# Stacked router logits, expert 3's second layer moved up, and a reordered fill and first round

## The reference, cut to what matters

```python
x = x + _L0_gnn_ref(_layernorm(x), adj, W, a)     # elu(softmax(mask(leaky(f_i + f_j))) @ (x @ W))
x = x + _L0_ffn_ref(_layernorm(x), ...)           # six experts of three layers, top 2 by a router
x = x + _L1_gnn_ref(_layernorm(x), adj, W, a)
x = x + _L1_ffn_ref(_layernorm(x), ...)           # eight experts, routed by graph; then a layernorm
```

```python
rh = relu(features @ router_w1 + router_b1)                  # 128 -> 64
expert_logits = softmax(rh @ router_w2 + router_b2)          # 64 -> 6
top_w, top_i = top_k(expert_logits, 2)
routing_weights = softmax(top_w)
h1 = relu(einsum('bsd,edh->bseh', features, expert_w1) + expert_b1)
h2 = relu(einsum('bseh,ehf->bsef', h1, expert_w2) + expert_b2)
expert_out = einsum('bsef,efo->bseo', h2, expert_w3) + expert_b3
```

## Time and profile before

| | us |
|---|---|
| median of 3 runs (583.07 to 584.28) | 583.71 |
| the profiled execution | 578.58 |
| its span in the trace | 576.8 |

### The profile page before, as it was taken

The page is one execution under the profiler, slowest core; times in us unless marked ns, Lnnn a source line. Parts: engine busy times, 40 slices in busy tenths (PEclk is TensorE's granted clock), DMA queues, the critical chain, the costliest instruction groups (busy, mean ns, idle before and its releaser), DMA issues.

```text
span 576.8 us, 14978 instructions
## 1 busy us (share of the span) xinstructions
PE 541.0 (94%) x3752; PEld 448.3 (78%) x3784; DVE 451.5 (78%) x1664; ACT 417.7 (72%) x1097; POOL 228.9 (40%) x441
## 2 busy tenths in 40 slices
PE   6678999999999999999999999999987999999993
PEld 5556678787777887878777787867765799999993
DVE  3866969889898888989889897786557387877777
ACT  1355667878878787887878878786663678888883
POOL 5112214442443434334442434413313045666664
PEclk8899999999999999999999999999999899999998
DMA  8504325042340513415043250321320467887732
GB/s 205 121 15 151 99 67 167 3 165 71 96 151 13 165 44 121 125 39 165 11 153 88 77 165 2 110 70 44 110 74 2 145 206 221 260 259 221 219 114 73
DMA packets 78833, 66.44 MB, mean 115 GB/s; under 512 B 9916, under 2 KB 64460, under 8 KB 78796
## 3 DMA queue, kind: packets, MB, share of 16 engines
q1 hardware_dynamic: 65562, 60.60, 34.4%
q10 hardware_dynamic: 13234, 5.42, 3.5%
HBM read 61.57 MB, written 4.42 MB: 114 GB/s over the span
## 4 chain that ended last, share of the span: by engine, by line
PE 79%; issue 6%; DVE 5%; POOL 4%; ACT 3%; ACTq 1%; DMA 1%; DVEq 0%; POOLq 0%; SPq 0%
PE bank L1566 14%; PE bank L1553 13%; PE wide L206 5%; PE bank L1848 5%; PE wide L1848 4%; PE bank L1858 4%; PE wide L1858 4%; PE wide L239 4%; PE bank L1545 3%; PE bank L1546 3%; PE bank L1547 3%; PE wide L231 2%; PE wide L1594 2%; PE wide L199 2%; PE wide L220 2%
## 5 line engine op out<-in xcount | busy, mean ns | idle before, releaser
L1566 PE MATMUL bank<-w,h2w 128*128 128x128 f32 x768 | 104.2, 279 | 2.6 <-DVE h2w L1130 2.6
L1566 PEld LDWEIGHTS bank<-w,h2w 128*128 128x128 f32 x768 | 94.8, 192 | 7.9 <-DVE h2w L1130 4.0
L1553 PE MATMUL bank<-h,w 128*128 128x512 f32 x192 | 98.8, 596 | 0.3 <-ACT h L846 0.3
L841 ACT ACTIVATE h<-bank,b 128x512 f32<-128x512 f32 x96 | 66.2, 689 | 42.2 <-PE bank L1553 42.2
L846 ACT ACTIVATE h<-bank,b 128x512 f32<-128x512 f32 x96 | 65.9, 687 | 12.8 <-PE bank L1547 12.6
L1130 DVE TENSOR_TENSOR h2w<-h,wide_w 128x512 f32<-128x512 f32 x96 | 64.8, 676 | 8.0 <-ACT h L841 7.8
L1545 PE MATMUL bank<-xnTh,w1h 128*128 128x512 f32 x96 | 67.0, 698 | 0.0
L100 POOL TENSOR_TENSOR route_var_eps<-route_mean_var,eps 128x4 f32<-128x4 f32 x17 | 11.2, 659 | 117.5 <-DVE route_mean_var L93 117.3
L100 POOL TENSOR_TENSOR at_var_eps<-at_mean_var,eps 128x4 f32<-128x4 f32 x32 | 12.4, 387 | 95.4 <-DVE at_mean_var L93 95.2
L268 ACT ACTIVATE at_pr<-at_lk,at_nm 128x128 f32<-128x128 f32 x124 | 40.0, 415 | 1.7 <-DVE at_nm L303 1.5
L206 PE MATMUL wide<-at_wc,at_xT 128*128 128x130 f32 x248 | 34.8, 286 | 4.2 <-ACT at_xT L247 4.2
(11 more groups left out here) (304 smaller groups left out, 1363.6 us busy)
## 6 DMA issues: line engine op xcount, KB each, us to landing
wide_w<-w_scratch SPq DMA_DIRECT2D x96, 256.0 KB, 4.5
mask<-in_L_ffn_W SPq DMA_DIRECT2D x124, 128.0 KB, 2.4
x<-in_x SPq DMA_DIRECT2D x16, 256.0 KB, 5.4
adj_in<-in_adj SPq DMA_DIRECT2D x16, 256.0 KB, 6.0
wide_w<-bmix_scratch SPq DMA_DIRECT2D x16, 256.0 KB, 3.5
xin<-in_x SPq DMA_DIRECT2D x15, 256.0 KB, 5.8
out<-at_pr ACTq DMA_DIRECT2D x8, 256.0 KB, 2.8
out<-at_prT ACTq DMA_DIRECT2D x7, 256.0 KB, 2.9
```

Of the source, the lines that this page charges most:

```text
L841: a.activation(h2[:, e % 2, :], b_h2[:, :], ACT.Relu, bias=b2[:, e:e + 1]).then_inc(h2_ready, 1)
L1553: pe.matmul(b_h2[:, :], w2[:, e, :], h1[:, e % 2, :], start=True, stop=True).then_inc(l2_done, 1)
L1566: last = pe.matmul(b_out[:, s], h2w[:, e % 2, s], w3[:, e, :], start=False, stop=(e == E0 - 1), skip_group_check=True)
```

## The change

**Logits of stacked tiles.** The first router weights now stand twice side by side (128 columns instead of 64), so the hidden layer comes out twice, on partitions 0 to 63 and 64 to 127. `route_relu` takes tiles 0 and 1 from the lower half and tiles 2 and 3 from the upper half, in two activations of 64 by 256 instead of one of 64 by 512. rh then holds two tiles one above the other in 128 rows by 256 columns, and rw2 has the second weights twice on its diagonal with zeros beside them, so `route_logits` needs two products of 12 columns instead of four of 6. The second bias is no longer a row of rh; VectorE adds it in a new first step of `route_first` (`lgb`). The later steps count one more, which renumbers their semaphore values.

**Second layer of expert 3.** TensorE's `layer2(n + 3, 3)` moves from behind the transposes of the probabilities to a place between the logits and them, in every round from i0 = 1.

**Fill.** The router of group 0 starts earlier: `route_transpose` moves ahead of the rows of group 1's attention and its hidden layer is cut into a high and a low part, the high one ahead of the scores; it writes to another bank (b_out). The unread products in round -1 become 28, 5, 2 and 8 instead of 12, 3, 3 and 0. VectorE places the bias rows of two tiles in `split_b3` and of the other two (`place_b3(2, GG)`) behind the first `norm_apply` of the router. ScalarE's `relu2(0)` of group 0 moves behind the elu.

**First round.** Experts run ahead of each other in another order: `layer3(0)`, `layer2(2)`, `layer1(3)`, `layer3(1)` come before the scores of group 2, and `weigh(2)` and `weigh(3)` come earlier on VectorE. VectorE's statistics of group 1 for the router move ahead of the rescaling of the projection, and GpSimd's root of them ahead of the splits.

**Transfers.** b2, w2 and w3 move from ScalarE's queue to SyncE's, behind b3 and ahead of the late weights. ScalarE issues two more small ones (rb1 and the second router weights twice), and waits before them for a memset of rw2 by GpSimd.

The diff, cut; left out are the new shapes of the tiles, the semaphore counts, and the lines of round 0 and of the other engines that only follow the words above:

```diff
-            sp.wait_ge(b3_zero, 1)
+            sp.wait_ge(b3_zero, 2)
             for q in range(3):
                 sp.dma_start(b3[32 * q:32 * q + KW, :],
                              A["L0_ffn_expert_b3"].unsqueeze(1).broadcast_to([E0, GG, P])).then_inc(small_loaded, 16)
+            with nc.allow_non_contiguous_dma(reason="bias columns, once"):
+                sp.dma_start(b2[:, :], A["L0_ffn_expert_b2"].rearrange("e p -> p e")).then_inc(small_loaded, 16)
+            sp.dma_start(w2[:, :, :], A["L0_ffn_expert_w2"].rearrange("e d h -> d e h")).then_inc(small_loaded, 16)
+            sp.dma_start(w3[:, :, :], A["L0_ffn_expert_w3"].rearrange("e d h -> d e h")).then_inc(small_loaded, 16)
...
+            p.memset(rw2[:, :], 0.0).then_inc(b3_zero, 1)
...
+                if i0 == 0:
+                    norm_root(rn, p, eps, minus_half, 1, rn["xn_ready"])
                 if live("attn0", i0) and i0 != -LEAD["attn0"]:
                     attn_pool_split(at0, p, zero, i + 2)
-                if i0 == 0:
-                    norm_root(rn, p, eps, minus_half, 1, rn["xn_ready"])
...
-                a.dma_start(rb1[:, :], A["L0_ffn_router_b1"].unsqueeze(1)).then_inc(small_loaded, 16)
-                a.dma_start(rw2[0:RH, :], A["L0_ffn_router_w2"]).then_inc(small_loaded, 16)
-                a.dma_start(rw2[RH:RH + 1, :], A["L0_ffn_router_b2"].unsqueeze(0)).then_inc(small_loaded, 16)
+                a.wait_ge(b3_zero, 1)
+                for q in range(2):
+                    half = slice(q * RH, (q + 1) * RH)
+                    a.dma_start(rb1[half, :], A["L0_ffn_router_b1"].unsqueeze(1)).then_inc(small_loaded, 16)
+                    a.dma_start(rw2[half, q * E0:(q + 1) * E0], A["L0_ffn_router_w2"]).then_inc(small_loaded, 16)
+                a.dma_start(rb2[:, :], A["L0_ffn_router_b2"].partition_broadcast(P)).then_inc(small_loaded, 16)
                 a.dma_start(b1[:, :], A["L0_ffn_expert_b1"].rearrange("e p -> p e")).then_inc(small_loaded, 16)
                 a.dma_start(h2[:, 0, 0:RH], A["L0_ffn_router_w1"]).then_inc(raw_loaded, 16)
                 a.dma_start(h1[:, :, :].rearrange("p a f -> p (a f)")[:, 0:E0 * P],
                             A["L0_ffn_expert_w1"].rearrange("e d h -> d e h")).then_inc(raw_loaded, 16)
-                a.dma_start(b2[:, :], A["L0_ffn_expert_b2"].rearrange("e p -> p e")).then_inc(small_loaded, 16)
-                a.dma_start(w2[:, :, :], A["L0_ffn_expert_w2"].rearrange("e d h -> d e h"))\
-                    .then_inc(small_loaded, 16)
-                a.dma_start(w3[:, :, :], A["L0_ffn_expert_w3"].rearrange("e d h -> d e h"))\
-                    .then_inc(small_loaded, 16)
...
-                    a.activation(rh[0:RH, :], b_misc[0:RH, :], ACT.Relu, bias=rb1[:, :]).then_inc(rh_ready, 1)
+                    for q in range(2):
+                        half = slice(q * RH, (q + 1) * RH)
+                        part = a.activation(rh[half, :], of[half, lane[q]], ACT.Relu, bias=rb1[half, :])
+                    part.then_inc(rh_ready, 1)
...
-                    relu2(0, 0)
...
                 if i0 == -LEAD["route"]:
+                    relu2(0, 0)
                     relu1(1, 1)
                 elif live("experts", i0, 1):
                     relu1(n + 6, 0)
...
-                for t in range(GG):
+                place_b3(0, 2)
+
+            def place_b3(first, end):
+
+                for t in range(first, end):
                     v.tensor_scalar(b3x[0:64, t, :], b3h[0:64, :].bitcast(F32), rowtile[0:64, t:t + 1], None, ALU.mult)
                     v.tensor_scalar(b3x[64:KB, t, :], b3l[64:KB, :], rowtile[64:KB, t:t + 1], None, ALU.mult)\
                         .then_inc(split_step, 1)
...
-                lg = b_misc[:, 0:GG * E0].rearrange("p (t e) -> p t e", t=GG)
-                v.tensor_reduce(lgmx[:, :], lg, AX, ALU.max).then_inc(route_step, 1)
+                lg = b_misc[:, 0:GG * E0].rearrange("p (q h e) -> p h q e", q=2, h=2)
+                v.tensor_tensor(lgb[:, :, :].rearrange("p (h q) e -> p h q e", h=2), lg,
+                                rb2[:, :].unsqueeze(1).unsqueeze(1).broadcast_to([P, 2, 2, E0]), ALU.add)\
+                    .then_inc(route_step, 1)
                 v.wait_ge(route_step, base + 1)
-                v.tensor_tensor(lgd[:, :, :], lg, lgmx[:, :].unsqueeze(2).broadcast_to([P, GG, E0]),
+                v.tensor_reduce(lgmx[:, :], lgb[:, :, :], AX, ALU.max).then_inc(route_step, 1)
+                v.wait_ge(route_step, base + 2)
+                v.tensor_tensor(lgd[:, :, :], lgb[:, :, :], lgmx[:, :].unsqueeze(2).broadcast_to([P, GG, E0]),
                                 ALU.subtract).then_inc(route_step, 1)
 
...
+                if i0 == 0:
+                    measure(rn, 1, at0["x_ready"], 2)
+                    weight_low(0)
...
                 if i0 == 0:
-                    measure(rn, 1, at0["x_ready"], 2)
-                    weight_low(0)
...
+                if i0 == -LEAD["route"]:
+                    place_b3(2, GG)
...
+                if i0 == 0:
+                    weigh(3, 0, 3)
...
                 pe.wait_ge(xnTh_ready, g + 1)
+                pe.matmul(to[:, :], rw1h[:, :], xnTh[:, par, :], start=True, stop=False)
+                pe.matmul(to[:, :], rw1l[:, :], xnTh[:, par, :], start=False, stop=False)
+
+            def route_hidden_low(g, par, to=b_misc):
                 pe.wait_ge(xnTl_ready, g + 1)
-                pe.matmul(b_misc[0:RH, :], rw1h[:, :], xnTh[:, par, :], start=True, stop=False)
-                pe.matmul(b_misc[0:RH, :], rw1l[:, :], xnTh[:, par, :], start=False, stop=False)
-                pe.matmul(b_misc[0:RH, :], rw1h[:, :], xnTl[:, par, :], start=False, stop=True)\
...
             def route_logits(g):
                 pe.wait_ge(rh_ready, g + 1)
-                for t in range(GG):
-                    last = pe.matmul(b_misc[:, t * E0:(t + 1) * E0], rh[:, t * P:(t + 1) * P], rw2[:, :],
-                                     start=True, stop=True)
+                for q in range(2):
+                    last = pe.matmul(b_misc[:, q * 2 * E0:(q + 1) * 2 * E0], rh[:, q * P:(q + 1) * P], rw2[:, :],
+                                     start=True, stop=True, skip_group_check=True)
...
+                if i0 == 0:
+                    layer1(2, 0, 0, 2)
+                    bias3(0)
+                    layer3(0, 0)
+                    layer2(2, 2)
+                elif run:
+                    layer1(n + 1, i, par, 1)
...
                         pe.wait_ge(spread_step, 6)
-                    busy_fill(i0, 12)
+                    busy_fill(i0, 12 if i0 == -LEAD["attn0"] else 28)
+                    if i0 == -LEAD["route"]:
+                        route_transpose(i, i0)
                     attn_pe_rows(at0, pe, identb, i + 2)
-                    busy_fill(i0, 3)
-                if route and i0 != 0:
+                    busy_fill(i0, 3 if i0 == -LEAD["attn0"] else 5)
+                if route and i0 >= 0:
                     route_transpose(i, i0)
+                if i0 == -LEAD["route"]:
+                    route_hidden_high(0, 0, b_out)
+                    busy(b_pool, 2)
...
-                        layer1(0, 0, 1 - par, 0)
-
-                if run:
+                if route and i0 >= 0:
+                    pe.wait_ge(xnTl_ready, i + 2)
+                    route_hidden_high(i + 1, 1 - par)
+                    route_hidden_low(i + 1, 1 - par)
+                if i0 == -LEAD["route"]:
+                    route_hidden_low(0, 0, b_out)
+                    layer1(0, 0, 1 - par, 0)
+
...
                 if route:
                     route_logits(i + 1)
+                if i0 == 0:
+                    layer3(2, 2)
+                    layer2(4, 4)
+                if run and i0 > 0:
+                    layer2(n + 3, 3)
...
-                    busy_fill(i0, 16 if i0 == -LEAD["attn0"] else 0)
+                    busy_fill(i0, 16 if i0 == -LEAD["attn0"] else 8)
                     attn_pe_transpose_probs(at0, pe, ident, i + 2)
                     busy_fill(i0, 3)
 
-                if run:
-                    layer2(n + 3, 3)
+                if run and i0 > 0:
                     layer1(n + 4, i, par, 4)
```

131 lines of the change are left out of this document (68 added, 63 removed).

## The result

| | us |
|---|---|
| changed kernel, median of 16 runs (575.74 to 582.93) | 577.47 |
| kernel before, the 16 runs beside them (578.20 to 584.28) | 579.65 |
| ratio | 0.9946, interval 0.9923 to 0.9970 |

The account below looks back on a forecast made before the run. Steady rounds were taken as bound by TensorE's queue and a chain through ScalarE and VectorE arriving together, the fill by waits. First round -2.8, thirteen rounds -0.3, last round -0.4: 583.7 - 3.5 = 580.2 us, range 576.6 to 583.3.

Parts of the forecast that it names:

- the -2.8 for fill and first round: Fill through first round: earlier copies, exponentials and reordered experts bring the end of the first round 2.8 us earlier.
- the 583.7: Starting level: median of the runs of the kernel before, 5.1 us above its profiled execution, from which 3.5 was subtracted.
- The logits: Steady round, TensorE: two stacked products instead of four cost 0.41 of 0.81 us, so 0.40 goes.
- The two halves: Steady round, ScalarE: splitting the router's activation adds at most 0.15 us, hidden under a cover of 0.3 to 0.4.
- the second layer: Steady round: expert 3's second layer ahead of the transposes delays them by 0.86 us; 0.02 of the saved 0.40 remains.
- the 1.0: Start, ScalarE: with three issues moved away, the first copy starts at 8.00 instead of 9.05, 1.0 us earlier.
- 1.65 at the first mean: Fill, group 0: the front's 1.0 and four bias-row calls moved behind start VectorE's mean at 21.14 instead of 22.79.
- p_sum's 0.73 instead of 2.7: First round, VectorE: p_sum forecast at 54.4 instead of 57.06, 2.7 us earlier.
- Its own sign for being wrong: Prediction wrong if rounds get shorter than 24.3 us, or if the fill gains under 1.5 with the clock up.
- The second: Rival, fill: a low-clock stretch on the 28 unread products, or late bias rows, leaves 1.5 gain; 581.9 us; 20 in 100.
- The third: Rival, rounds: logits pair as long as four makes the exponential 0.35 later in each of 13; 585.1 us; 6 in 100.
- The first: Rival, rounds: copy and exponential keep their distance to TensorE's shortened queue, 0.35 gained each; 575.6 us; 12 in 100.

Follow-up runs that it names:

- l2_back: Changed kernel with expert 3's second layer put back behind the transposes of the probabilities from i0 = 1; 582.14 us, ratio to the kernel before 1.0013.
- l2_only: Kernel before with only expert 3's second layer moved up between logits and transposes from i0 = 1; 586.42 us, ratio 1.0099.
- rounds_only: Kernel before with stacked logits and expert 3's second layer moved up alone; loads, fill and first round as before; 584.60 us, ratio 1.0084.
- xn_first: Changed kernel with the router's normalising of group 1 ahead of the weighing of expert 1 in the first round; 577.82 us in its one execution.
- tail_busy: Changed kernel with more unread products behind the rounds; 576.47 us, ratio to the kernel before 0.9939.
- weigh3_early: Changed kernel with VectorE's weighing of expert 3 ahead of the ranking in every round; 575.64 us, ratio to the kernel before 0.9921.

## Why the prediction was right or wrong

Two steps failed: the -2.8 for fill and first round, which was 0.87 in the changed kernel's profile (the first full round's logits start at 75.64, 77.29 and 77.05 in its three profiles, and at 76.51, 77.82 and 76.71 in three with the fill of before), and the 583.7 that the sum was put on, where the kernel before has 579.65. The two errors have opposite signs. That 577.47 lies within 576.6 to 583.3 is luck, and so is that the ratio of the first comparison comes near the forecast's.

**The level.** I noted that the profiled execution lay 5.1 under the median and put the forecast on the median. The kernel before is mostly at 578 to 580, and the difference that I forecast, -3.5, on that level gives 576; the measured median is 577.47.

**A steady round.** The sum was right by luck (0.02 forecast, 0.03 measured; distance 7.04; a new wait of 0.30 where I said 0.37), since its terms were not. The logits gave 0.45, not 0.40. The two halves cost 0.40, not 0.15, and the cover for them, named as 0.3 to 0.4, was 0.19 at most even behind the moved layer: the exponentials end at 223.51 and the transposes start at 223.70. Because of that the second layer costs nothing where I charged 0.86 for it. l2_back, forecast by the same terms, came out 0.78 a round beside the forecast. The Trainium skill's price for the halves (ScalarE: Activation LUTs, "What ACT_TABLE_LOAD costs"; the estimate from it was 0.19 more) is near the 0.14 on the same partitions; for the stacked halves the measured 0.40 decides. The last round gave 0.47 (0.4 forecast). The 24.55 of the prediction runs from the first product of a row of logits to the last one of another; from first to first it is 24.49, and 24.53 in a middle round.

**The start.** I took the 1.0 from a queue that ends earlier, and from transposes that end at 8.00 as in the profile of before. In the changed kernel's three profiles they end at 9.06, because TensorE takes 1.02, 1.21 and 1.09 for products that took 0.61, 0.71 and 0.63. The granted clock's record shows 1.00 there; the durations show half the speed. All seven other profiles of the kernel before and its variants are slow like this too (transposes at 7.92 to 7.97); the one that I had, with 7.37, was the exception. Thus of 1.65 at the first mean 0.47 to 0.90 was left, the part from the bias rows (0.65 between l2_only, 22.54, and the changed kernel, 21.89, whose copies start within 0.04). Why TensorE starts at full speed in four of sixteen profiles is open. The Trainium skill's sentence on issuing engines (DMA: Bandwidth & Descriptors, "Issuing engines are not separate DMA queues") says that the sequencer's time, which is all that is saved, is usually small beside the transfer itself. For this copy the saving is nothing. In rounds_only the issue of w3 took 2.68 us, where the transfer of the first layers, of the same 384 KB, took 6.6 from issue to landing, and the first copy paid 4.0 for the issues.

**The fill's order.** The terms up to group 1's statistics were right to 0.2: the charge of 1.0 for the scores was 1.17, the exponential's 1.17 was 1.19 and the swap's 1.2 was 1.16.

**The first round.** What I left out is expert 1's weights: their chain through DRAM starts with the weights of group 0, which came only 0.25 earlier, and VectorE waited 0.76 for them ahead of r_xn. Together with the 1.0 missing from the fill (0.40 where 1.41 was forecast) that is p_sum's 0.73 instead of 2.7. xn_first took most of that wait away, and at most 0.2 of it came through to p_sum, so removing it would not have given the 2.7. What would is shown by tail_busy: with no slow product and no low stretch p_sum comes 3.17 and the next logits 3.33 ahead of the kernel before, some 2.2 of it by the change. So the order was worth nearly what was forecast, and the assumption of a TensorE at full speed did not hold. Its own sign for being wrong, a fill that gains under 1.5 with the clock up, is what the profile showed.

**Rivals.** The second (the fill gives most back, 1.5 left) is the nearest in size, but not by its mechanism: no low stretch fell on the 28 unread products in any profile. The third decided from a pair of logits of 0.71; it takes 0.36. The first had the rounds gain 0.35; they gain 0.03, and even with VectorE's order mended (weigh3_early) 0.14. Two of their sums were off: the first adds the rounds' 0.3 a second time (576.0, not 575.6), the second leaves out the last round's 0.4 (581.5, not 581.9).

## What to carry to other kernels

Count a split instruction on its own engine with the work behind it, down to the wait of the engine that takes that work; here TensorE's 0.45 and ScalarE's 0.40 were the two sides of one edit, and a second edit that looked like a cost was what hid them. Where executions of one kernel fall on two levels, find the stretch that separates them before adding a difference to a median. And about 50 unread products in the idle time ahead of a dense stage can take away executions that are 6 us longer, at no measured cost to the others.

## What the runs showed of the hardware

- Two activations of 64 by 256 (ScalarE) take 0.71 us from start to start on the same partitions and 0.97 when the second is on partitions 64 to 127; one of 64 by 512 takes 0.57.
- The issue of one transfer of 384 KB (w3) on ScalarE took 0.89 to 2.17 us in five profiles with the same transfers ahead of it, and 2.68 in the one profile with two more small ones ahead.
- TensorE's products can run at half speed where the record of the granted clock shows 1.00: in the changed kernel from 5.9 to about 14 us (projection 2.07 against tail_busy's 1.13, both at 1.00). The profile of the kernel before has the same 2.07 with a recorded 0.58.
- Products in otherwise idle time of TensorE behind the rounds kept the granted clock at 1.00 from 428 to 468, where without them the clock was at 0.50 for some 3 to 21 us of it.
